# A graph network of five residual steps on one core: skip products, first-half features, lead-in fillers and load slots put elsewhere

## The reference, cut to what matters

```python
h = relu(layernorm(x)); x = x + gat(h, adj, W0, a0)      # attention layer 0
h = relu(layernorm(x)); x = x + gat(h, adj, W1, a1)      # attention layer 1
h0 = relu(layernorm(x))                                  # layers 2 and 3, and the joining layer
h1 = 0.2 * h0 + 0.8 * gat(h0, adj, W2, ...)
h2 = 0.2 * h0 + 0.8 * gat(h1, adj, W3, ...)
x = x + concat(h0, h1, h2) @ mlp_w + mlp_b
h = relu(layernorm(x)); x = x + last(h, adj, w_k, w_q)   # softmax attention, Taylor series of a @ a

def gat(h, adj, W, a):          # 2048 nodes, 64 features
    Wh = h @ W
    e = leaky_relu((Wh @ a_src)[:, None] + (Wh @ a_dst)[None, :])
    return elu(softmax(where(adj > 0, e, -9e15), axis=1) @ Wh)
```

## Time and profile before

| what | value |
|---|---|
| median of 3 timed runs | 585.03 us (584.64 to 595.99) |
| the profiled execution, its own time | 580.28 us |
| its span, first to last instruction | 578.4 us |
| mean granted TensorE clock, share of full | 0.988 |
| TensorE busy | 529.5 us |
| VectorE / ScalarE / GpSimd busy | 380.3 / 263.3 / 30.2 us |

### The profile page before, as it was taken

How to read it: one execution, slowest core, us unless ns; L and a number is a source line. 1 busy time by engine, 2 the same in 40 slices (tenths; PEclk the granted TensorE clock), 3 DMA queues, 4 the chain that set the end, 5 groups by cost and what they waited for, 6 DMA issues and landing times.

```text
span 578.4 us, 7918 instructions
## 1 busy us (share of the span) xinstructions
PE 529.5 (92%) x3300; PEld 202.4 (35%) x3300; DVE 380.3 (66%) x551; ACT 263.3 (46%) x297; POOL 30.2 (5%) x32
## 2 busy tenths in 40 slices
PE   6888987998998998998888999999889999999997
PEld 5422222343223343323233223245334344333332
DVE  4888689548979637989765989637977983100000
ACT  3479964534665543665543755444234772000000
POOL 3300000211000100000100000021100000000000
PEclk9879999999999999999999999999999999999999
DMA  8977000000000000000000000000000000000000
GB/s 309 409 280 275 4 1 1 0 2 1 1 0 1 2 0 2 1 1 0 1 1 2 0 2 1 0 1 1 1 1 1 0 1 2 0 1 1 0 19 18
DMA packets 5635, 19.43 MB, mean 34 GB/s; under 512 B 608, under 2 KB 608, under 8 KB 5600
## 3 DMA queue, kind: packets, MB, share of 16 engines
q1 hardware_dynamic: 5600, 18.93, 8.9%
HBM read 18.40 MB, written 0.52 MB: 33 GB/s over the span
## 4 chain that ended last, share of the span: by engine, by line
PE 63%; DVE 23%; ACT 6%; issue 4%; DMA 3%; POOL 1%; SPq 0%; DVEq 0%; ACTq 0%
PE PROD L793 11%; DVE X L1361 10%; PE X L1062 10%; PE PROD L1062 9%; PE X L785 7%; PE S L813 6%; ACT big L471 4%; DMA big<-in_adjT 3%; PE X L1053 2%; DVE tops L1625 2%; DVE big L1373 2%; PE M L648 1%; DVE nadj L1475 1%; PE M L747 1%; DVE big L1370 1%
## 5 line engine op out<-in xcount | busy, mean ns | idle before, releaser
L471 ACT ACTIVATE big<-X,v 128x1024 f32<-128x1024 f32 x128 | 141.6, 1114 | 100.5 <-PE X L785 100.1
L1361 DVE SCALAR_TENSOR_TENSOR X<-wB,v,aB 128x1024 f32<-128x1024 f32 x128 | 163.4, 1293 | 27.6 <-ACT big L471 26.3
L793 PE MATMUL PROD<-big,Wh 128*64 128x512 f32 x512 | 134.3, 605 | 1.9 <-ACT big L471 1.7
L785 PE MATMUL X<-nadj,bigI 128*64 128x512 bf16 x512 | 77.9, 383 | 19.6 <-DVE X L1361 19.3
L785 PEld LDWEIGHTS X<-nadj,bigI 128*64 128x64 bf16 x512 | 25.3, 109 | 102.3 <-DVE X L1361 73.2
L813 PE MATMUL S<-big,onesf 128*32 128x512 f32 x400 | 53.3, 604 | 2.4 <-DVE big L1373 2.4
L793 PEld LDWEIGHTS PROD<-big,Wh 128*64 128x64 f32 x512 | 31.1, 136 | 52.2 <-issue 30.3
L1062 PE MATMUL PROD<-big,Wh 128*64 128x512 f32 x128 | 30.6, 594 | 0.0
L528 ACT ACTIVATE big<-nadj 128x1024 fp8e4<-128x1024 bf16 x26 | 26.3, 1053 | 9.0 <-DVE nadj L1475 9.0
L398 POOL TENSOR_TENSOR rr<-var,mhalf 128x8 f32<-128x8 f32 x8 | 14.5, 1818 | 298.7 <-DVE var L1222 298.7
L1062 PE MATMUL X<-big,Wh 128*64 128x512 f32 x128 | 28.6, 595 | 0.0
(11 more groups left out here) (307 smaller groups left out, 597.2 us busy)
## 6 DMA issues: line engine op xcount, KB each, us to landing
big<-in_adjT SPq DMA_DIRECT2D x28, 512.0 KB, 7.5
aB<-in_adjT SPq DMA_DIRECT2D x4, 512.0 KB, 7.5
cst<-in_cst SPq DMA_DIRECT2D x1, 537.0 KB, 7.5
x<-in_xT SPq DMA_DIRECT2D x1, 512.0 KB, 3.7
out<-x SPq DMA_DIRECT2D x2, 256.0 KB, 2.0
late<-in_late SPq DMA_DIRECT2D x1, 272.5 KB, 5.8
cst<-in_cst SPq DMA_DIRECT2D x1, 263.0 KB, 2.8
```

The lines of the kernel that those rows point to most:

```text
L471: act.activation(prob[:, t % U, :], X[t % 2][:], ACT.Exp, bias=v2[l % 2][:, k:k + 1]).then_inc(p_ready, 1)
L785: last = pe.matmul(X[t % 2][feat(side), hh * BANK:(hh + 1) * BANK], bigI[:, feat(side)], nadj[:, k, half_cols(c, hh)], start=False, stop=T ...
L793: last = pe.matmul(PROD[c][feat(hh), :], Wh[l % 2][:, k, :], prob[:, t % U, hh * BANK:(hh + 1) * BANK], start=k == 0, stop=k == NB - 1)
L1361: dve.scalar_tensor_tensor(X[t % 2][:], wB[:, cols(c)], v8[l % 2][:, k:k + 1], aB[:, cols(c)], ALU.max, ALU.add).then_inc(x_written, 1)
```

## The change

It has five parts.

- **Load slots.** Half 1's blocks go round slots 7, 8, 0, 1, 2, 3, 4, ... instead of 7, 8, 4, 5, 6 over and over.
- **Lead-in and first half of layer 0.** Two fillers stand behind each of the level products of blocks 9, 10, 12 and 13, and two more ahead of the first mask. In pair 5 of half 0 the last two level products stand ahead of the row sums, and `shift_products(0, 2, 4)` behind them; it stood in pair 6.
- **Gaps behind layers 0 and 1.** The next layer's `features` of half 0 leave pair 6 for a place behind `centre`; on VectorE their scaled copies, levels and row parts go behind `variance`. `w_rows` and all level products stand behind the features of half 1, and `w_broadcast` goes behind `top_levels`. In the last pair the products of step 14 stand ahead of the sums and those of step 15 ahead of `total`.
- **Joining layer.** h0 and h1 are multiplied early (`skip_terms`) into a bank of their own, and `skip_rows` adds that and the bias to x: for c = 0 in the gap ahead of layer 3, for c = 1 behind `top_levels` and after the second exponent of layer 3, in the place of 9 of 17 fillers. `mlp` and `mlp_rows` are left with h2's part.
- **Gap ahead of layer 3, and layer 2.** The features of half 1 stand ahead of the last five level products, with 3 fillers in the place of 4. In layer 2 `root_broadcast(0)` goes behind the shift products, and `input_rows(0)` behind the second exponent.

A rewritten `by_dve` and a `convert` in the place of `mask_words` give the same instructions as before. The new semaphore and the new function `skip_bank` (X1's upper bank for c = 0, M for c = 1) are left out below, and so is ScalarE's order, where `w_row` of the next layer now follows `square` instead of standing ahead of it.

```diff
@@ -284,7 +285,7 @@
         ADDS = 4
-        SLOT_OF = [n % SLOTS for n in range(NB)] + [(7, 8, 4, 5, 6)[j % 5] for j in range(NB)]
+        SLOT_OF = [n % SLOTS for n in range(NB)] + [(7, 8, 0, 1, 2, 3, 4, 5, 6, 7, 8, 4, 5, 6, 7, 8)[j] for j in range(NB)]
@@ -738,24 +742,29 @@
                 pe.wait_ge(level_ready, 2 * l + 1)
-                pe.wait_ge(wB_ready, 2 * (2 * l + 1))
+                if l in (0, 3):
+                    pe.wait_ge(wB_ready, 2 * (2 * l + 1))
                 for jb in range(CB if l else 0, NB):
...
                         chunk_levels(0, jb)
+                        if jb in (9, 10, 12, 13):
+                            repeat(X[1][:, BANK:CH], 2)
                         continue
...
                     last.then_inc(top_psum, 1)
-                if l == 2:
-                    root_broadcast(0)
-                elif l:
+                if l in (1, 2):
+                    w_broadcast(2 * l)
+                if l:
                     repeat(X[0], 4)
...
                 shift_products(l, 0, 4 if l else 2)
+                if l == 2:
+                    root_broadcast(0)
@@ -774,6 +783,8 @@
                 for q in range(lo, hi):
+                    if l in (1, 2) and q == 2:
+                        pe.wait_ge(wB_ready, 2 * (2 * l + 1))
                     rows = slice(WIN * q, WIN * (q + 1))
@@ -833,14 +844,19 @@
                 n = NCH * 3 + c
-                pe.wait_ge(ld_late, 16)
                 pe.wait_ge(p_copied, n + 1)
-                for k, src in enumerate((h0, h1)):
-                    pe.matmul(EB[c][:], mw[:, k, :], src[:, c, :], start=k == 0, stop=False)
                 pe.wait_ge(t_ready, n + 1)
-                pe.matmul(EB[c][:], mw[:, 2, :], tb, start=False, stop=False)
+                pe.matmul(EB[c][:], mw[:, 2, :], tb, start=True, stop=False)
                 pe.wait_ge(e_ready, n + 1)
                 pe.matmul(EB[c][:], mw[:, 2, :], eo, start=False, stop=True).then_inc(mlp_psum, 1)
+
+            def skip_terms(c):
+
+                pe.wait_ge(ld_late, 16)
+                pe.wait_ge(h0_ready, c + 1)
+                pe.wait_ge(h_ready, c + 1)
+                pe.matmul(skip_bank(c), mw[:, 0, :], h0[:, c, :], start=True, stop=False)
+                pe.matmul(skip_bank(c), mw[:, 1, :], h1[:, c, :], start=False, stop=True).then_inc(skip_psum, 1)
@@ -900,12 +916,16 @@
                 w_rows(2 * l + 1)
-                repeat(M, 17 if l else 8)
+                if l == 3:
+                    skip_terms(1)
+                    repeat(PROD[0], 8)
+                else:
+                    repeat(M, 17 if l else 8)
                 if l == 0:
...
                     w_broadcast(1)
-                    repeat(PROD[0], 4)
+                    repeat(PROD[0], 6)
                 pe.wait_ge(nv_ready, 4 * (l + 1) if l else 2)
@@ -915,26 +935,34 @@
                         if c and p == NB // 2 - 1:
+                            if l < 2:
+                                products(l, c, k)
                             pe.wait_ge(p_ready, NB * (NCH * l + c + 1))
                             sums(l, c, k + 1)
-                            products(l, c, k)
-                            total(l, 1)
-                            products(l, c, k + 1)
+                            if l < 2:
+                                products(l, c, k + 1)
+                                total(l, 1)
+                            else:
+                                products(l, c, k)
+                                total(l, 1)
+                                products(l, c, k + 1)
                             continue
...
                             products(0, 0, k + 1)
-                            if p == 6:
+                            for i in range(2):
+                                if p < NB // 2 - 1:
+                                    mask(0, 0, k + 2 + i)
+                                else:
+                                    mask(0, 1, i)
+                            if p == 5:
+                                chunk_levels(1, NB - 2)
+                                chunk_levels(1, NB - 1)
+                            sums(0, 0, k + 1)
+                            for jb in range(4 + k if p else 2, 6 + k if p < 5 else 0):
+                                chunk_levels(1, jb)
+                            if p == 5:
                                 shift_products(0, 2, 4)
-                            if p < NB // 2 - 1:
-                                mask(0, 0, k + 2)
-                                mask(0, 0, k + 3)
-                            sums(0, 0, k + 1)
-                            for jb in range(4 + k if p else 2, 6 + k if p < 6 else 0):
-                                chunk_levels(1, jb)
-                            if p == NB // 2 - 1:
-                                mask(0, 1, 0)
-                                mask(0, 1, 1)
                             continue
@@ -963,9 +991,8 @@
                                 reach_spread()
-                            if p == 6:
-                                if l == 2:
-                                    pe.wait_ge(reachsq_ready, 1)
+                            if p == 6 and l == 2:
+                                pe.wait_ge(reachsq_ready, 1)
                                 features(2 * l + 2)
@@ -980,24 +1007,23 @@
                 reciprocal_rows(l, 1)
-                if l < 3:
-                    w_rows(2 * l + 2)
                 if l < 2:
                     centre_old(2 * l + 3)
-                    early_levels(l + 1, 0, 2)
                     centre(2 * l + 3)
+                    features(2 * l + 2)
+                    variances(2 * l + 3)
+                    features(2 * l + 3)
+                    repeat(X[0], 2)
+                    early_levels(l + 1, 0, CB)
+                    w_rows(2 * l + 2)
+                if l == 2:
+                    w_rows(2 * l + 2)
+                    early_levels(l + 1, 0, 3)
+                    skip_terms(0)
                     w_broadcast(2 * l + 2)
-                    variances(2 * l + 3)
-                    early_levels(l + 1, 2, 4)
                     features(2 * l + 3)
-                    early_levels(l + 1, 4, CB)
-                    repeat(X[0], 2)
-                if l == 2:
-                    early_levels(l + 1, 0, 3)
-                    w_broadcast(2 * l + 2)
                     early_levels(l + 1, 3, CB)
-                    features(2 * l + 3)
-                    repeat(X[0], 4)
+                    repeat(X[0], 3)
             def key_block(c, t, b, side=slice(0, P)):
@@ -1414,10 +1440,14 @@
             def mlp_rows(c):
+                dve.wait_ge(mlp_psum, c + 1)
+                ins = dve.tensor_tensor(x[:, c, :], x[:, c, :], EB[c][:], ALU.add)
+                signal(ins, x_new, 2 * 2 + c + 1)
+
+            def skip_rows(c):
                 dve.wait_ge(ld_late, 16)
-                dve.wait_ge(mlp_psum, c + 1)
-                ins = dve.scalar_tensor_tensor(x[:, c, :], EB[c][:], mb, x[:, c, :], ALU.add, ALU.add)
-                signal(ins, x_new, 2 * 2 + c + 1)
+                dve.wait_ge(skip_psum, c + 1)
+                link(dve.scalar_tensor_tensor(x[:, c, :], skip_bank(c), mb, x[:, c, :], ALU.add, ALU.add))
@@ -1529,8 +1559,6 @@
                         mask_words(n)
-                if l == 2:
-                    input_rows(0)
                 if l == 1:
@@ -1556,7 +1584,10 @@
                     if k == 1 and l == 2:
+                        input_rows(0)
                         activated(1, 1)
+                    if k == 1 and l == 3:
+                        skip_rows(1)
                     if k == 11 and l == 2:
@@ -1595,13 +1626,13 @@
                             variance(6)
-                if l < 3:
+                if l == 2:
                     features(2 * l + 2)
...
                     row_parts(2 * l + 2)
-                else:
+                if l == 3:
                     norms(0)
@@ -1613,9 +1644,15 @@
                     activated(l, 1)
+                    skip_rows(0)
                 if l < 2:
                     clip(2 * l + 3)
+                    features(2 * l + 2)
                     variance(2 * l + 3)
+                    for i in range(2):
+                        feature_rows(2 * l + 2, i)
+                    block_levels(l + 1, 0, CB)
+                    row_parts(2 * l + 2)
                 if l < 3:
```

More of the change, by code:

```diff
@@ L236, in program @@
         mlp_psum = sem("mlp_psum")
+        skip_psum = sem("skip_psum")
         c2_psum = sem("c2_psum")
@@ L334, in by_dve @@
         def by_dve(n):
-            return n < NB and n % 3 == 0
+            return n % 3 == 0 if n < NB else False
         def copies_by_dve(n):
@@ L347, in again, with skip_bank @@
             return (M, PROD[0])[c]
+        def skip_bank(c):
+            return (X[1][:, BANK:CH], M[:])[c]
         def sums_of(n):
@@ L553, in _ @@
                     if l == 0 and k % 2 and k < 12:
```

(6 more changed lines are left out.)

6 lines of the change are left out of this document (2 added, 4 removed).

## The result

| | before | after |
|---|---|---|
| timed runs on one chip, median us | 584.84 (584.58 to 595.99, 4 runs) | 575.78 (574.55 to 576.04, 4 runs) |
| ratio, 95% interval | | 0.9842 [0.9823, 0.9862] |
| profiled execution, its own time | 580.28 | 575.99 |
| span, mean granted clock | 578.4, 0.988 | 574.2, 0.997 |

The ratio leaves out the one run of 595.99, which stood 1.9% above the others. The forecast was 579.0, its range 574.5 to 583.8. The time lies in the range, whose low end had allowed for a profile that stood 4.75 us under the median. It is 3.2 us under the forecast, and the gain is 9.1 us where 6.0 was expected. The two profiled executions differ by only 4.3. Both gaps between the numbers have to be explained.

What follows compares the result with a forecast made beforehand. TensorE, busy 92% of the span, was taken to bound the kernel. Terms -1.3 - 1.6 + 0 - 0.8 - 1.8 - 0.5 sum to -6.0 us: 574.3 in a profile, 579.0 as median, range 574.5 to 583.8.

Steps and rivals of the forecast that it cites:

- lead-in, to the first target: Lead-in: fillers hold the clock, shift products deliver sooner, first target moves from 38.31 to 37.0; -1.3 us, bounds 0 and -2.5.
- halves of layer 0: Half to half in layer 0: earlier levels and shift products remove waits, next half's products start sooner; -1.6 us, bounds -1.0 and -1.8.
- first gap: Gap behind layer 0: centring 1.5 us earlier, then given back to moved steps, levels and broadcast; +0.1, bounds -0.6 and +0.5.
- second gap: Gap behind layer 1: root broadcast leaves `aB`'s way, but 17 fillers end when they did; -0.1, bounds -0.6 and +0.5.
- gap ahead of layer 3: Skip products fit TensorE's 1.99 us idle time and features pass 20 level records; -0.8 us, other cases -0.6 and 0.
- joining, half 0: Joining products of half 0, from 367.88 with no idle ahead: skip products' 1.8 us leave the path; -1.8, at worst -1.0.
- joining, half 1: Half 1's h2 product can start when its operand is ready, 395.36 instead of 395.94; -0.5 us, bounds 0 and -0.6.
- this cover holds: Lead-in: new slots start VectorE's second block transfer four microseconds earlier, so its 0.56 us wait does not delay the target.
- second rival: The gaps pay: VectorE's ten steps and TensorE's levels run shorter, each gap gives 0.6 or a little more; 577.6, chance 0.2.
- third rival: Joining layer's gain comes back: TensorE meets VectorE or ScalarE, skip products push the broadcast, half is lost; 580.9, chance 0.1.
- The fourth: Slower: clock falls in the first two gaps and ahead of layer 3; three falls cost 9.6, 588.6 us; chance 0.05.
- first rival: Clock falls anyway in the lead-in, whose long idle stretch stays; lead-in worth 0, fillers cost up to 0.5; 580.5, chance 0.2.

Runs made afterwards that it cites:

- changed again: The changed kernel, unchanged, timed and profiled again on a second chip; 574.89 us against 582.31 for before, ratio 0.9873.
- experiment 7: Kernel before with seven fillers in TensorE's idle time ahead of the broadcast to layer 3, nothing else; 580.78 us against 582.31, ratio 0.9971.
- experiment 5: The changed kernel, unchanged, timed again on the chip of the next three runs; 574.89 us against 582.31 for before, ratio 0.9873.
- experiment 8: Kernel before with the ten lead-in fillers alone, on the old load slots and old order of pairs; 581.33 us against 582.31, ratio 0.9982.

## Why the prediction was right, and where not

Stages against the first profile of before, in us:

| term | forecast | first profile after | changed again | by itself |
|---|---|---|---|---|
| lead-in, to the first target | -1.3 | -0.59 | -1.25 | -1.25 (with the pairs) |
| halves of layer 0 | -1.6 | -1.89 | -1.89 | -1.90 |
| first gap | +0.1 | +0.17 | +0.16 | +0.18 |
| second gap | -0.1 | -0.09 | -0.05 | +0.09 |
| gap ahead of layer 3 | -0.8 | -0.62 | -0.62 | not tried |
| joining, half 0 | -1.8 | -1.72 | -1.71 | -1.72 |
| joining, half 1 | -0.5 | -0.46 | -0.47 | -0.47 |
| sum | -6.0 | -5.2 | -5.83 | |
| start of the first levels | 0 | +0.99 | +0.73 | |
| in the profile | -6.0 | -4.2 | -5.1 | |

**The terms hold.** Seven stages of the second profile add up to 5.83 us against 6.0. The gap ahead of layer 3 is the one term that no run tried by itself. Lead-in: the fillers held the clock and `aB` set the target, as worked out. "The slots alone are worth nothing" was right word for word, and "this cover holds" was the slots' real part: without them the fillers give 0.67. Halves: 0.3 more than forecast and 0.1 beyond the bound of -1.8. Up to the next half's third mask the gain is 1.5 for 1.6; the 0.37 at the later wait for VectorE had not been looked at. Gaps: the chain ran as described, to 0.2 (centring -1.44 for -1.5, half 1's score parts -0.28 for -0.47, target +0.17 for +0.17), and the second rival's 0.6 is ruled out. Layer 3: `top_levels` came 0.70 earlier for 0.8, and `skip_rows(1)` did not quite fall into its wait (0.08). The third rival, the joining gain lost at a hop, is ruled out too. The fourth priced a fall of the clock at 3.2 us; those in the traces cost 1.0 to 1.6 each in the gap and in the last layer. Two sums of the prediction don't follow from its own terms, and nothing rests on them: the bad ends add up to -1.0, not -1.4, and half of the joining layer's 2.3 lost gives 580.2, not 580.9.

**The step that failed** is one outside the sum: "I carry the difference over unchanged", the 4.75 us between the profiled execution and the median. It isn't a constant of the kernel. For the changed kernel it is -0.2, and for the kernel before on the three chips of the experiments 2.0 to 2.7 (medians of 582.31 to 582.94, less 580.28). A part of it is the start of the first levels, 0.2 to 0.9 later in all five other traces with the old lead-in than in the first profile. For the rest, executions of the kernel before have clock holes that the profiled one had not, and the change fills two of the places where they begin.

- At 33 to 42 us: five of the six kernels with the old lead-in had a hole beginning near 33.5 us in their trace, and none of the eight with the fillers. In two of the fillers' eight it fell elsewhere, from 28.7 us or 43.1 us on, and the sixth kernel with the old lead-in (experiment 7) had it at 27.1 and 44.1 instead; its first target was 0.8 us earlier than in the first profile by that alone. That is the half of the first rival that was true, in the very first profile of the changed kernel, and its hole at 28.7 us cost the 0.66 by which its lead-in fell short.
- At 304 us: 1.59 to 1.63 us in three of six. Filling that idle time alone gave 1.5 us of median. The prediction had counted the fill as cover for the skip products, and had written of this place "TensorE idled 1.99 us in that gap without a fall", from one execution.
- At 405 to 415 us: 1.6 and 1.03 us in two of the eight traces of kernels built on before, none in six of the changed kernel's. The change touches nothing there, and two in eight against none in six may be chance.

The medians of experiment 5 fell by 7.4 us (582.31 to 574.89), and 5.8 of them are the stages. The other 1.6 are about what holes at these places cost, and the joining layer and the seven fillers, which fill the place at 304 us, each have 1.3 to 1.5 more in the median than in their stages. That is an argument from sizes: no run shares the 1.6 out. The first measurement's 9.1 came with a before of 584.84, 1.9 to 2.5 above the medians of the three chips, and no run shows why.

The rule that the prediction weighed fares better than it did there. In the gap ahead of layer 3 the clock fell right behind an idle stretch of 1.99 us, and it held where the stretch was filled. The Trainium skill, page "TensorE: Matmul & The Clock Gate", section "Why this matters for your kernels", puts such falls down to idle gaps between bursts of matmuls, though to longer ones than this; here the measurement decides. But the fall came in three executions of six. In the lead-in the one at 33 us went when the thin stretch was filled and the longer idle one, of 2.2 to 2.5 us, left alone. That idle stretch is a danger of its own all the same: two of the fourteen traces have a fall at its end, at 28.7 us in the first profile of the changed kernel and at 27.1 us in experiment 7.

## What to carry to other kernels

A sum of stages from one trace can be good to a few tenths of a microsecond and the median still miss it, when the executions differ by clock holes: profile the kernel before twice or more, and mark each place where the clock fell in any of them. An idle stretch of TensorE can then cost more than it waits. Moving a chain's head forward gives nothing as long as what it jumped over is queued on the engines that the chain needs next.

## What the runs showed of the hardware

- The same kernel, unchanged, ran between 580.42 and 585.2 us in twelve runs on one chip, at a mean granted clock of 0.976 to 0.994. The two slowest had 0.976, but the two quickest had 0.988, and so had two of 583.38: where the clock falls counts as well as for how long.
- A fall to half rate lasted about 3 to 10 us. In the gap ahead of layer 3 and in the last layer it delayed the end by 1.0 to 1.6 us; at 43.1 us in experiment 8 it delayed nothing.
- Two 32-row shift products on separate groups of rows, fp32 and 512 columns wide, took 1.13 us together at full clock and 2.08 at half. Four of them took no longer than two, 1.14 us, in the first gap of the kernel before:

```profile
133.14 1.14 PE L778 MATMUL X<-gridz,c 32*128 32x512 f32 x8
```
